# Graph attention on one core: x1 kept in SBUF, outputs written once, second layer reordered

## The reference, cut to what matters

```python
h = relu(layernorm(x))
x = x + gat(h, adj)          # layer 1: 16 heads of 32 features
h = relu(layernorm(x))
x = x + gnn(h, adj)          # layer 2

def gat(h):                  # masked softmax over neighbours, per head
    seq = (h @ W_seq).reshape(N, 16, 32)
    s = leaky_relu(seq @ a1 [:, None] + seq @ a2 [None, :], 0.2) + (1 - adj) * -65500
    return elu(softmax(s) @ seq @ W_out + b_out)

def gnn(h):
    q, k, v = h @ W_q.T + b_q, h @ W_k.T + b_k, h @ W_v.T + b_v
    z = (q @ k.T) / sqrt(512) * adj
    z = where(z == 0, -10000, z)
    return relu(softmax(z) @ v)
```

## Time and profile before

| | us |
|---|---|
| median of 3 runs | 493.81 |
| the profiled execution, its own time | 495.05 |
| its span in the trace | 493.1 |
| granted TensorE clock, mean | 0.921 |
| PE / DVE / ACT / POOL busy | 393.8 / 368.7 / 244.2 / 260.5 |
| first block, to the branch | 0 to 123 |
| sixteen heads | 123 to 217 |
| layer 1's tiles | 217 to 363 |
| layer 2's tiles, first gather to last scatter issued | 363.0 to 476.8 |

### The profile page before, as it was taken

One profiled execution on the slowest core, in us unless ns is written; L12 is line 12 of the kernel. 1 busy time (PEld: TensorE's weight loads), 2 busy tenths in 40 slices (PEclk: granted clock), 3 DMA queues, 4 the chain that ended last, 5 costly groups with the idle time before them and its releaser, 6 DMA issues.

```text
span 493.1 us, 6193 instructions
## 1 busy us (share of the span) xinstructions
PE 393.8 (80%) x2044; PEld 283.2 (57%) x2044; DVE 368.7 (75%) x728; ACT 244.2 (50%) x511; POOL 260.5 (53%) x267
## 2 busy tenths in 40 slices
PE   3599999994699998988499888879974738995960
PEld 3578888783488787873366555537562315542420
DVE  2998899983899998974999996997434539988300
ACT  1369877753899997923234333534423132242310
POOL 2343152246886886648466648554257766761330
PEclk9689999999699998999799999989995959898995
DMA  7968999510001333326334427512236766654450
GB/s 270 406 208 288 416 329 340 203 68 5 5 7 22 90 95 89 93 78 211 113 109 141 145 76 206 186 68 86 86 122 197 185 157 149 130 112 57 57 70 4
DMA packets 27259, 70.03 MB, mean 142 GB/s; under 512 B 8153, under 2 KB 8409, under 8 KB 25049
## 3 DMA queue, kind: packets, MB, share of 16 engines
q0 software_dynamic: 13056, 38.45, 29.6%
q1 hardware_dynamic: 13904, 31.16, 17.7%
q10 hardware_dynamic: 264, 0.00, 0.0%
HBM read 52.47 MB, written 17.13 MB: 141 GB/s over the span
## 4 chain that ended last, share of the span: by engine, by line
POOL 21%; DVE 18%; issue 18%; PE 12%; DMA 2%; ACT 1%; DVEq 0%; POOLq 0%; ACTq 0%
POOL s_shared L1210 7%; PE psum L1372 6%; PE psum L1277 4%; POOL out_dram L1221 4%; DVE s_shared L786 3%; DVE s_shared L779 3%; DVE s_shared L777 3%; POOL s_rs L1220 3%; POOL s_shared L1230 2%; DVE w_seq L968 2%; DVE s_x L793 2%; POOL s_x L1226 2%; POOL s_shared L1191 2%; DVE h_t L1012 1%; DMA w_out<-h_dram,s_near_rank 1%
## 5 line engine op out<-in xcount | busy, mean ns | idle before, releaser
L1047 ACT ACTIVATE s_shared<-psum,seq_all 128x320 bf16<-128x320 f32 x192 | 81.7, 567 | 13.4 <-PE psum L1257 7.3
L1277 PE MATMUL psum<-s_shared 128*128 128x198 bf16 x768 | 76.5, 257 | 11.4 <-POOL s_shared L1191 11.4
L1277 PEld LDWEIGHTS psum<-s_shared 128*128 128x128 bf16 x768 | 69.0, 99 | 19.6 <-POOL s_shared L1191 10.4
L547 PE MATMUL psum<-w_seq,hT 128*128 128x272 f32 x256 | 63.0, 401 | 0.4 <-ACT w_seq L414 0.4
L1299 PE MATMUL psum<-w_out,hT 128*128 128x512 f32 x128 | 58.8, 603 | 0.0
L1321 PE MATMUL psum<-w_qk,s_early 128*128 128x257 f32 x240 | 55.7, 385 | 0.0
L547 PEld LDWEIGHTS psum<-w_seq,hT 128*128 128x128 f32 x256 | 48.8, 195 | 10.1 <-ACT w_seq L414 0.5
L1321 PEld LDWEIGHTS psum<-w_qk,s_early 128*128 128x128 f32 x240 | 45.3, 194 | 6.4
L1210 POOL DMA_INDIRECT s_shared<-seq_dram,tab x30 | 36.9, 1232 | 13.7 <-issue 8.9
L266 POOL TENSOR_TENSOR rstd<-veps,power 128x1 f32<-128x1 f32 x16 | 8.9, 559 | 60.8 <-DVE veps L458 60.8
L1191 POOL TENSOR_TENSOR s_shared<-s_shared 128x1056 f32<-128x1056 f32 x16 | 31.1, 1945 | 16.3 <-DVE s_shared L779 16.2
(11 more groups left out here) (253 smaller groups left out, 758.1 us busy)
## 6 DMA issues: line engine op xcount, KB each, us to landing
adj_ring<-in_adj_dram SPq DMA_DIRECT2D x16, 1024.0 KB, 7.6
seq_dram<-seq_all POOLq DMA_DIRECT2D x16, 264.0 KB, 4.2
x_ring<-in_x_dram SPq DMA_DIRECT2D x16, 256.0 KB, 8.2
h_dram<-h_t SPq DMA_DIRECT2D x16, 256.0 KB
w_seq<-in_L_gnn_W_seq_dram SPq DMA_DIRECT2D x1, 1024.0 KB, 7.2
w_q<-in_L_gnn_W_q_dram SPq DMA_DIRECT2D x1, 1024.0 KB, 13.8
w_k<-in_L_gnn_W_k_dram SPq DMA_DIRECT2D x1, 1024.0 KB, 16.0
w_v<-in_L_gnn_W_v_dram SPq DMA_DIRECT2D x1, 1024.0 KB, 9.6
```

What stands on the lines that cost most here:

```text
L547: last = pe.matmul(bank[2 + 2 * (t % 2) + i][:, 0:SX // 2], hT[:, t % 2, c * P:(c + 1) * P], w_seq[:, c, i * (SX // 2):(i + 1) * (SX // 2) ...
L1047: last = act.activation(ind[i][:, j, PAD:], bank[4 + i][:, 0:LN], ACT.Sign, bias=seq_all[:, j, D + n:D + n + 1])
L1277: last = pe.matmul(acc(i)[:, k, 0:3 * W2], ind[i][:, j, k * P:(k + 1) * P], rhs.rearrange("p t w -> p (t w)"), start=(j == 0 and k != 1), ...
```

## The change

1. **Start.** `a_row` takes a1 and a2 as two short rows on one partition; PE spreads them to all partitions with one matmul (`a_spread`) and DVE picks each partition's entry into `a_col` (`a_set`). PE runs 8 matmuls on a zero tile before that one and 8 behind it (`WARM`, `WARM_2`), and 8 more at the head of the second block (`WARM_3`).
2. **Scatters.** The record scatters leave the first block; all 16 are issued in heads 0 to 7, two a head. The early rows and x tiles start at head 9, and only 4 x tiles are early; the others come in layer 1's loop (`X_LATE`).
3. **Layer 1's loop.** The scatter of x1 to `out` is gone; `GATHER` is rearranged, and a ninth gather goes ahead of the loop.
4. **Layer 2.** Tiles go in the order `SEQ1`, 0, 1, 2, 3, 4, 6, 8, 10, 12, 14, 11, 13, 15, 9, 7, 5, in four parts. x1 stays in SBUF, so the gathered rows get other places (`row`), and row k from the 13th on is gathered only after k - 11 dots. ACT's `output` is gone: DVE adds the relu of the product onto x1 in place (`add_x`), and POOL scatters each finished tile once, without accumulating, after all gathers. PE makes the queries of tiles 12 to 15 before the first product. `products(t)` now waits for `add_x(t - 4)`.

```diff
+GATHER = {0: ((7, 1, 4),), 1: ((7, 4, 5), (9, 0, 2)), 2: ((9, 2, 4), (11, 0, 1)), 3: ((11, 1, 3),),
+          5: ((12, 0, 2),), 6: ((14, 0, 2),), 7: ((13, 0, 3),), 8: ((15, 0, 3),)}
+X_LATE = {0: (4,), 1: (5,), 2: (6,), 3: (7,), 6: (8, 9), 7: (10, 11), 8: (12, 13), 9: (14,), 10: (15,)}
+WARM = 8
+WARM_2 = 8
+SEQ1 = [0, 1, 2, 3, 4, 6, 8, 10, 12, 14, 11, 13, 15, 9, 7, 5]
+EXP1_AT = {2: 1, 4: 2, 10: 3}
+BASES_AT = {0: (4,), 3: (5, 6), 4: (7,), 5: (8,), 6: (9,), 7: (10,), 8: (11,), 9: (12,), 11: (13, 14), 12: (15,)}
+X_EARLY = 4
...
-                pool.wait_ge(lone_set, 1)
-                pool.wait_ge(rank_ready, 2)
-                for t in range(SCATTERED):
-                    pool.indirect_dma_start(record_dram[:, :], bass.IndirectOffsetOnAxis(rank[:, t:t + 1], 0),
-                                            record[:, t, :], None).then_inc(rec_stored, 16)
...
-                    act.dma_start(a_col[:, k:k + 1],
-                                  a_d.rearrange("(d o) -> d o", o=1).partition_broadcast(P // DH)).then_inc(a_loaded, 16)
+                    act.dma_start(a_row[:, k, :], a_d.rearrange("(o d) -> o d", o=1)).then_inc(a_loaded, 16)
...
+                pe.wait_ge(warm_set, 1)
+                for _ in range(WARM):
+                    pe.matmul(bank[6], warm[:, 0:P], warm[:, :])
+                pe.wait_ge(const_ready, 1)
+                pe.wait_ge(a_loaded, 2 * 16)
+                pe.matmul(bank[7][:, 0:2 * DH], ones[0:1, :], a_row[:, :, :].rearrange("p k d -> p (k d)")).then_inc(a_spread, 1)
+                for _ in range(WARM_2):
+                    pe.matmul(bank[6], warm[:, 0:P], warm[:, :])
...
-                    if n < 5:
-                        scatter(SCATTER[n], SCATTER[n + 1])
-                    if n == 6:
+                    if n < T // 2:
+                        scatter(2 * n, 2 * n + 2)
+                    if n == AHEAD_FROM:
...
-                gather(5, 0, SLOTS[5])
+                gather(5, 0, 8)
+                gather(7, 0, 1)
...
-                    pool.indirect_dma_start(out[:, :], bass.IndirectOffsetOnAxis(own[:, SEQ[t], :], 0), x1[:, t, :], None).then_inc(x1_stored, 16)
...
                 def gather1(t):
                     for s in range(SLOTS[t]):
-                        pool.indirect_dma_start(row(FIRST_SLOT[t] + s), None, h1_dram[:, :],
+                        k = ROW1[t] + s
+                        if k >= ROWS_AHEAD:
+                            pool.wait_ge(dot_done, k - ROWS_AHEAD + 1)
+                        if k == ROWS_EARLY:
+                            pool.wait_ge(u_done, U_NO[EARLY - 1] + 1)
+                        if k == ROWS_AGAIN:
+                            pool.wait_ge(agg_ready, 4)
+                        pool.indirect_dma_start(row(t, s), None, h1_dram[:, :],
...
-                def put(t):
-                    pool.wait_ge(o_ready, t + 1)
-                    pool.indirect_dma_start(out[:, :], bass.IndirectOffsetOnAxis(own[:, t, :], 0),
-                                            o_t[t % 4], None, compute_op=ALU.add).then_inc(out_stored[t % 4], 16)
...
-                for t in range(9):
+                for t in SEQ1:
                     gather1(t)
-                for t in range(T):
-                    put(t)
-                    if 9 + t < T:
-                        gather1(9 + t)
...
+                for p in range(T):
+                    t = SEQ1[p]
+                    pool.wait_ge(o_added, p + 1)
+                    pool.indirect_dma_start(out[:, :], bass.IndirectOffsetOnAxis(own[:, t, :], 0),
+                                            x1[:, TURN[t], :], None).then_inc(out_stored, 16)
...
+                def add_x(p):
+                    own_x = x1[:, TURN[SEQ1[p]], :]
+                    dve.wait_ge(o_done, p + 1)
+                    dve.scalar_tensor_tensor(own_x, bank[2 + p % 4], 0.0, own_x, ALU.max, ALU.add).then_inc(o_added, 1)
...
+                constants(0, EARLY)
+                for t in range(4):
+                    dot(t)
+                scores1(0)
                 dve.wait_ge(h_sum_mm, 1)
                 dve.tensor_copy(h_sum, bank[0]).then_inc(sums_ready, 1)
...
+                for t in (6, 8, 10, 12):
+                    dot(t)
+                constants(EARLY, T)
+                dot(14)
+                scores1(1)
+                dot(11)
+                dot(13)
+                normalise1(1)
+                aggregate1(6)
+                aggregate1(8)
+                dot(15)
+                scores1(2)
+                aggregate1(10)
+                normalise1(2)
+                add_x(0)
+                add_x(1)
+                aggregate1(12)
+                add_x(2)
+                dot(9)
+                aggregate1(14)
+                add_x(3)
+                dot(7)
+                aggregate1(11)
+                add_x(4)
+                dot(5)
+                scores1(3)
+                aggregate1(13)
+                add_x(5)
+                normalise1(3)
+                aggregate1(15)
+                add_x(6)
+                aggregate1(9)
+                add_x(7)
+                aggregate1(7)
+                add_x(8)
+                aggregate1(5)
+                for p in range(9, T):
+                    add_x(p)
...
                 for k in range(T):
                     act.wait_ge(a_tr, k + 1)
                     if k >= 2:
                         act.wait_ge(o_done, k - 1)
                     act.activation(aT[k % 2], bank[k % 2], ACT.Copy).then_inc(aT_done, 1)
...
+                    if k in EXP1_AT:
+                        exp_scores1(EXP1_AT[k])
+                    for p in BASES_AT.get(k, ()):
+                        if p in FIRSTS:
+                            act.wait_ge(weights_ready, FIRSTS.index(p) + 2)
+                        base_of(p)
...
+                for _ in range(WARM_3):
+                    pe.matmul(bank[2], ones_b[:, :], bias_rows[:, 0, 0:D])
...
                 def products(t):
                     pe.wait_ge(aT_done, t + 1)
                     if t >= 4:
-                        pe.wait_ge(o_ready, t - 3)
+                        pe.wait_ge(o_added, t - 3)
...
                 for k in range(1, T):
-                    if k in first_of:
+                    if k in FIRSTS:
                         products(k - 1)
                         transposes1(k)
                     else:
                         transposes1(k)
                         products(k - 1)
```

More of the change, by code:

```diff
@@ L167, in build @@
         a_col = sb("a_col", [P, 2], stack=first)
+        a_row = sb("a_row", [1, 2, DH], stack=first)
+        own_dim = sb("own_dim", [P, DH], stack=first)
+        a_own = sb("a_own", [P, 2, DH], stack=first)
+        warm = sb("warm", [P, 512], BF16, stack=first)
         own_head = sb("own_head", [P, C, H], stack=first)
@@ L248, in _ @@
             def _(pool):
+                pool.memset(warm[:, :], 0.0).then_inc(warm_set, 1)
                 pool.memset(ones[:, :], 1.0).then_inc(const_ready, 1)
@@ L473, in search_index @@
                     dve.max_index(record[:, t, 0:TOP], near[:, t, :], adj_ring[:, t % AR, :]).then_inc(adj_searched, 1)
+                dve.wait_ge(const_ready, 2)
+                step(dve.tensor_reduce(own_dim[:, :], ident[:, :].rearrange("p (q d) -> p d q", d=DH), AX_X, ALU.add))
                 ln(0)
                 ln_bias(0)
+                dve.wait_ge(a_spread, 1)
+                step(dve.tensor_tensor(a_own[:, :, :], bank[7][:, 0:2 * DH].rearrange("p (k d) -> p k d", k=2),
+                                       own_dim[:, :].unsqueeze(1).to_broadcast([P, 2, DH]), ALU.mult))
+                dve.tensor_reduce(a_col[:, :], a_own[:, :, :], AX_X, ALU.add).then_inc(a_set, 1)
                 ln(1)
@@ L974, in constants, with bc @@
                     step(dve.tensor_tensor(zp[:, lo:hi, :], pen[:, lo:hi, :], zc[:, lo:hi].unsqueeze(2).to_broadcast([P, hi - lo, TOP]), ALU.add))
-                def bc(a, t0, n):
-                    return a[:, t0:t0 + n].unsqueeze(2).to_broadcast([P, n, TOP])
+                def bc(a, g):
+                    return a[:, PARTS[g]].unsqueeze(2).to_broadcast([P, PART_TILES[g], TOP])
                 def scores1(g):
-                    t0, n = PARTS[g]
-                    zz, qq, m = z[:, t0:t0 + n, :], zq[:, t0:t0 + n, :], zm[:, t0:t0 + n]
-                    for t in range(t0, t0 + n):
-                        dot(t)
-                    if t0 == EARLY:
-                        constants(EARLY, T)
+                    part = PARTS[g]
+                    zz, qq, m = z[:, part, :], zq[:, part, :], zm[:, part]
                     dve.wait_ge(dot_done, dots[0])
-                    step(dve.tensor_tensor(zz, zz, zp[:, t0:t0 + n, :], ALU.add))
+                    step(dve.tensor_tensor(zz, zz, zp[:, part, :], ALU.add))
                     step(dve.tensor_scalar(qq, zz, 0.0, NONE, ALU.is_equal, ALU.mult))
@@ L1005, in normalise1 @@
```

(14 more changed lines are left out.)

145 lines of the change are left out of this document (64 added, 81 removed).

## The result

The changed kernel takes 495.53 us (median of 20 runs, 492.62 to 498.77), the kernel before 493.84 (20 runs, 487.81 to 496.87); the ratio is 1.0063, with a 95% interval of 1.0037 to 1.0088. The forecast was 485.4. 495.53 lies just outside the range, and "slower" had been given 0.13. A median here is over all executions; a ratio and its interval leave out the slow ones, those over 1.5% above the fastest of the same kernel.

A forecast was written before the change was run, and what follows sets the result against it. The prediction saw no single bounding engine, but work handed round in fixed order, a chain of waits. -3.0 - 3.4 - 1.3 + 0.3 - 1.0 = -8.4 from 493.8 gave 485.4 us; range 476 to 495.5.

The forecast's parts named there:

- Start, -3.0: First block's start: first product at 20 to 23 instead of 26.03, taking 3.0 us off the block; bounds 0 and 6.
- the ring argument: First block: DVE's later waits for x, 1.87 and 1.60 us, come from SP's queue and go when PE starts earlier.
- Boundary, -3.4: End of first block: without POOL's record scatters ACT is last, at 116.9, so 3.4 us less; bounds -3.4 and 0.
- Head 0, -1.3: Second block's first head: eight warm matmuls make PE's first 36 matmuls take 3.39 us, not 4.73; bounds -1.3 and +0.5.
- Layer 1's loop, +0.3: Layer 1's tiles: +1.3 for a ninth gather ahead, -1.0 at turn 6, other turns 0; bounds -4 and +2.
- Layer 2, -1.0: Layer 2: 0.5 us from the walk and 0.5 from the last scatter's issue; bounds -11 and +8.
- The walk: Layer 2's written orders stepped through from 366.6 with average durations; last scatter issued at 476.3, before 476.80.
- rival 3: Layer 2: ACT's standstill comes again at a copy on the path, +8 us, 493.4; chance 14%.
- Rival 2: Layer 2: its two coupled waits are lost because adds are done in time, -10 us, 475.4; chance 13%.
- the coupled waits: Layer 2: DVE waits 6 and 6.5 us, behind products 4 and 9, which wait for late adds.
- Rival 5: Layer 2: POOL's gather issue is stretched by DVE's two-input instructions; at 1.8 us a row +10.8, 496.2; chance 9%.

The follow-up runs named there:

- b_start: Kernel before with only the change's start (a1 and a2 as rows spread by a product, sixteen warm products): 487.55 us, ratio 0.9909.
- a_adds: Changed kernel with the x adds earlier in DVE's layer 2 order, one about every product: 476.81 us, ratio 0.9668.
- a_pause14: Changed kernel with one POOL wait ahead of layer 2's row 14 until ACT has copied the first two transposed aggregates: 483.81 us, ratio 0.9821.
- b_pause16: Kernel before with only a POOL wait ahead of layer 2's row 16 until ACT has copied the third transposed aggregate: 489.34 us, ratio 0.9924.
- b_early: Kernel before with the change's start and record scatters in heads 0 to 7, old layer 2 and x1 scatters: 485.29 us, ratio 0.9876.
- a_adds_checks: Changed kernel with earlier adds and four POOL waits, ahead of layer 2's rows 12, 18, 22 and 26: 472.71 us, ratio 0.9582.
- a_half: Changed kernel with layer 2's gathers fetching half of each row, as many gathers and descriptors: 489.71 us in one run.
- a_adds_pause12: Changed kernel with earlier adds and one POOL wait ahead of layer 2's row 12 until ACT has copied the last of u: 471.40 us, ratio 0.9525.
- a_gap: Changed kernel with a one-column POOL memset, waited for, between any two gathers of layer 2: 494.14 us in one run.
- a_shift64: Changed kernel with eight already met waits ahead of each head's signs on ACT, 64 more instructions: 494.42 us, ratio 1.0055.
- a_pebusy: Changed kernel with 48 more 512-column products on PE after the transposes of layer 2's second tile: 506.82 us in one run.
- a_sp_rows: Changed kernel with layer 2's 40 rows fetched by plain SP DMAs of consecutive rows instead of POOL's gathers: 470.99 us in one run.

## Why the prediction was wrong, step by step

- **Start, -3.0.** Right in kind, too small: `b_start` gave 4.5 us (3.0 to 6.0, from its ratio). DVE's two waits for x behind 40 us are gone, 3.5 us, so the ring argument held. What the sum lacked is that DVE's first search began 1.5 us earlier (10.14 in `b_start`, 11.67 before), in both kernels behind the landing of the first adj tile; why it landed earlier no run shows. The first product came at 19.14, not at 20 to 23. I charged PE 4 to 8 us for warm products; of the first eight almost nothing was on the path, and without all sixteen the first product came 0.6 us later. With them PE's 16 transposes of W_seq took 1.91 us, without them 2.84; the 32 products on `a_mat` took 6.63 us (6.33 in the change) and 6.83, and in both cases the granted clock fell to 0.50 (1.2 GHz) under them.
- **Boundary, -3.4.** The second block began 10.5 us earlier, 4.1 more than start and boundary together were given: 4.9 by the start (`b_start`, 118.38) and 5.7 by the boundary. In `b_start` POOL's last scatter ended at 115.3 and the second block began at 118.38, 3.1 us later, as before; in the change ACT ended at 111.84 and it began at 112.73, 0.9 later. Of the 2.9 us that the sum kept as the cost of the boundary itself, some 2 go with POOL's scatters. What in them takes it, no run shows.
- **Head 0, -1.3.** Not seen there: its products took 4.95 us, at a granted clock that fell from 1.00 to 0.50 by 120 us, and 4.73 before. PE had stood 2.95 us behind the warm products, but that does not decide it: in `a_adds` PE stood as long, and the products took 3.38 us at 1.00. The heads as a whole gave 1.8, none of it at head 0, so that the sum came out near here is luck.
- **Layer 1's loop, +0.3.** It was +0.7. Right.
- **Layer 2, -1.0: the step that failed**, by 16 us. The walk let PE's signals arrive when PE was done: "PE finished product 3 at 395.5". In the trace this fourth product began only at 402.5 and ended at 406.1, although layer 2 had started 12 us earlier. This was rival 3, ACT's standstill, at 14% and 8 us. I had read it as something that falls on ACT at random and that copies with slack would hide. It is neither: it comes in all eleven profiles in which the first run of gathers has no break put in, it delays PE's signals, and here it fell on the first copies, on which everything in this order depends. Its price by the pause was 2.4%, 12 us, where the rival said 8. The rest of the walk held: in `a_pause14` DVE waited 6.48 us behind product 4 and 7.64 behind product 9 (forecast 6 and 6.5), and layer 2 took 116.1 us, where the walk says 113; if all of the pause were lost time, 116.1 - 4.3 = 111.8 us would be left, an estimate. That `a_pause14` comes to 0.9821 of 493.8, or 485.0, beside a forecast of 485.4, is partly luck: ahead of layer 2 the change gained 4.3 us more than forecast, and layer 2 with the pause took 3 us more.
- **Rival 2**, the coupled waits, was priced at 10 us. Earlier adds took 19.7 us off layer 2 (129.3 to 109.6). The two waits are 11.6 us of that (7.68 and 8.14 us in the change, 4.18 left). For the rest, one of DVE's three waits for products at the very end is gone (2.20 us), a loss that I had in the walk and did not put into the rival; what is left is not taken apart.
- **Rival 5**, the stretched issue, did not occur. Layer 2's first twenty gathers came (376.56 - 351.30)/19 = 1.33 us apart, as before.
- My baseline hid the mechanism. The kernel before had paid the hold as well (`b_pause16`: 0.8%; 6 us of layer 2 in `b_early`), so that rows of before looked like what the old order costs.

DVE's two coupled waits in `a_pause14`:

```profile
406.22 1.54 DVE L1041 SCALAR_TENSOR_TENSOR h_t<-s_shared,hT,h_t 128x512 f32<-128x512 f32 x2 [6.48 <-ACT h_t L1178]
...
435.75 0.16 DVE L1027 TENSOR_TENSOR hT<-hT,s_others 128x3 f32<-128x3 f32 x1 [7.64 <-ACT hT L1186]
```

## What to carry to other kernels

- A wait that the profile lays to "remote" or "issue", beside an engine whose input was ready long before, is a finding and not noise. Look at what else ran in that stretch in every profile you have, and take the lone cause away in one cheap run before you forecast around it.
- Where POOL is to issue more than a dozen gathers in a row while PE hands results on, try one wait of POOL for something that PE's signals must have achieved; four kernels gained 0.8 to 2.4% each by it. Three more waits behind the first gained nothing (`a_adds_checks`).
- When an engine in fixed order carries both the work and the release of buffers (here the adds), put each release directly where its input is due. Here that was worth 3.9%, more than any other edit.

## What the runs showed of the hardware

While POOL issued gathers one behind the other (0.95 us each, 0.3 between), PE's signals got through in time for the first 7 us (`a_half`) to 20 us (before) and then came up to 21 us late (27 for the second transposition). Where POOL stopped, those still held rose together: 1.4 us after the stop in `a_pause14`, 1.9 in `a_adds_pause12`, 2.7 in `a_half`, 2.8 in `a_gap`, 3.2 in `a_shift64`. But a stop is not needed. In the changed kernel POOL left no gap over 0.31 us from 351.3 to 388.15, and the signals came one by one, at 378.5 (by ACT's start), 387.60 and 393.24:

```profile
377.81 0.95 POOL L1299 DMA_INDIRECT w_out<-h_dram,s_near_rank  x1 [0.30 <-issue]
...
387.20 0.95 POOL L1299 DMA_INDIRECT bv_bc<-h_dram,s_near_rank  x1 [0.30 <-issue]
...
392.94 0.95 POOL L1299 DMA_INDIRECT s_early<-h_dram,s_near_rank  x1 [0.30 <-issue]
```

With more unsignalled work on PE, PE itself was slowed to a matmul in 1.41 us. As many bytes by plain DMAs of SP, at up to 288 GB/s, held nothing. So it is POOL's gathers and not the traffic. What in them does it, POOL's writing of descriptors or what the DMA engines do with them, no run here separates; plain DMAs also read consecutive rows. Nor do I know why holds return at some later places (389.0 and 400.6 in `a_adds_pause12`) and not at others: behind their pauses `a_pause14` ran 27 us and `b_pause16` 51 us of POOL's DMAs without one.

One rival is untested. Every execution on record has a span and a granted clock of its own, so each seems to have been traced. It may be the trace's own records of PE that pile up while POOL gathers; that would also explain why unsignalled products were slowed in `a_pebusy`, but no run tests it. Whether the hold, and the gain by a pause, exist where nothing is recorded stays open.

Two pages bear on this. The Trainium skill ("Perfetto Trace Analysis", summary of the profiler window per engine type) says that a matmul's window ends at an estimated end and leaves out the semaphore's propagation. The trace agrees: the signals rose outside the windows, mostly 0.02 us behind their ends, and here up to 27 us behind. The Trainium skill ("DMA: Bandwidth & Descriptors", SWDGE vs HWDGE vs iDMA) says that GpSimd writes the descriptors of its DMAs into rings in SBUF and that DMAs of SP do not take this path; that fits `a_sp_rows`, though no run shows the rings.
